# State scan of a four-layer convolution kernel: v*B on TensorE from diagonal images of B, the decay in SBUF

## What is computed

```
delta = softplus(dt_proj(x_proj(xi)) + bias)          # (2, 4, 192, 2304)
A     = -exp(A_log)                                   # (4, 192, 16)
h[n, l] = exp(delta[l] * A[n]) * h[n, l-1] + f(S[l], A[n]) * v[l] * B[n, l]
y[l]    = sum over n of C[n, l] * h[n, l]
```

## Time and profile before

| | us |
|---|---|
| median of three runs (2942.47 to 2949.4) | 2945.18 |
| span of the profiled execution, first to last instruction | 2938.3 |
| VectorE busy | 2503.6 |
| TensorE busy | 2263.7 |
| GpSimd busy | 1896.0 |
| ScalarE busy | 1743.5 |

### The profile page before, as it was taken

How to read it: one execution, slowest core, us unless ns; L and a number is a source line. 1 busy time by engine, 2 the same in 40 slices (tenths; PEclk the granted TensorE clock), 3 DMA queues, 4 the chain that set the end, 5 groups by cost and what they waited for, 6 DMA issues and landing times. The chain is left out here.

```text
span 2938.3 us, 27688 instructions
## 1 busy us (share of the span) xinstructions
PE 2263.7 (77%) x8714; PEld 1197.9 (41%) x8714; DVE 2503.6 (85%) x2085; ACT 1743.5 (59%) x2935; POOL 1896.0 (65%) x646
## 2 busy tenths in 40 slices
PE   6853677777877777787777778778984999799579
PEld 3421234343443434343443434444442555355444
DVE  5657999999999999999999999986787777699721
ACT  1566787878888888888878788863230000263220
POOL 0166999999999999999999999984000000198000
PEclk9967799999999999999999999998997999899689
DMA  1277445555454555545455554535005453100360
GB/s 48 88 219 272 102 112 137 130 124 130 115 133 118 131 136 123 129 112 132 119 131 134 125 129 112 135 90 191 0 0 143 110 129 104 43 8 8 82 89 24
DMA packets 145457, 323.07 MB, mean 110 GB/s; under 512 B 48219, under 2 KB 63840, under 8 KB 140320
## 3 DMA queue, kind: packets, MB, share of 16 engines
q1 hardware_dynamic: 144224, 317.17, 42.7%
q10 hardware_dynamic: 1088, 4.13, 0.6%
HBM read 234.46 MB, written 46.87 MB: 96 GB/s over the span
## 5 line engine op out<-in xcount | busy, mean ns | idle before, releaser
L903 POOL TENSOR_TENSOR l0c_r<-l0c_r,l0c_v 128x1536 f32<-128x1536 f32 x253 | 869.4, 3442 | 96.3 <-DVE l0c_r L862 96.3
L940 ACT ACTIVATE ps<-l0c_dlt,l0c_na 128x512 f32<-128x512 f32 (+1 forms) x1152 | 625.5, 574 | 286.5 <-DVE l0c_h L891 267.2
L912 POOL TENSOR_TENSOR l0c_hcp<-l0c_cb,l0c_h 128x1536 f32<-128x1536 f32 x216 | 743.2, 3446 | 5.5 <-DVE l0c_h L891 4.1
L891 DVE TENSOR_TENSOR_SCAN l0c_h<-ps,l0c_h,l0c_r 128x768 f32<-128x768 f32 x384 | 694.1, 1808 | 1.8 <-issue 1.2
L818 PE MATMUL ps<-l0c_hcp,net_ident 128*128 128x512 f32 x1728 | 645.2, 496 | 25.2 <-ACT l_Z L933 11.9
L950 ACT ACTIVATE l0c_r<-l0c_S,l0c_floor,l0c_na 128x768 f32<-128x768 f32 x576 | 579.9, 1014 | 0.1
L862 DVE SCALAR_TENSOR_TENSOR l0c_r<-l0c_r,ps 128x768 f32<-128x768 f32 x576 | 536.1, 931 | 18.1 <-issue 8.5
L752 PE MATMUL ps<-l0c_Bp,l0c_sel 96*128 96x512 bf16 x1012 | 256.0, 335 | 301.1 <-DVE l0c_hcv L869 146.1
L818 PEld LDWEIGHTS ps<-l0c_hcp,net_ident 128*128 128x128 f32 x1728 | 299.2, 193 | 297.6 <-issue 216.9
L891 DVE TENSOR_TENSOR_SCAN l0c_h<-ps,l0c_r 128x768 f32<-128x768 f32 x192 | 335.4, 1747 | 0.0
L1628 PE MATMUL ps<-l_prod,l_wa 128*96 128x384 f32 (+1 forms) x888 | 292.1, 493 | 25.7 <-DVE l_prod L1545 25.7
(11 more groups left out here) (280 smaller groups left out, 2739.9 us busy)
## 6 DMA issues: line engine op xcount, KB each, us to landing
l0c_cb<-cf SPq DMA_DIRECT2D x432, 384.0 KB, 5.5
l_other<-l_p SPq DMA_DIRECT2D x22, 864.0 KB, 6.0
dlt<-l0s_dl SPq DMA_DIRECT2D x36, 384.0 KB, 2.3
v<-l0s_vv SPq DMA_DIRECT2D x36, 384.0 KB, 2.9
l0c_dlt<-dlt SPq DMA_DIRECT2D x36, 384.0 KB, 3.6
l0c_v<-v SPq DMA_DIRECT2D x36, 384.0 KB, 4.4
l_other<-l_p SPq DMA_DIRECT2D x22, 288.0 KB, 6.7
l0c_Bp<-bc SPq DMA_DIRECT2D x36, 144.0 KB, 3.8
```

What stands on the lines that cost most here:

```text
L891: dve.tensor_tensor_scan(h[:, n, :], da[j % 2], r[:, j % NR, :], init, ALU.mult, ALU.add).then_inc(s_scan, 1)
L903: pool.tensor_tensor(two, two, v[:, (j // N) % 2, :].unsqueeze(1).to_broadcast([128, 2, SEG]), ALU.mult).then_inc(s_w, 2)
L912: pool.tensor_tensor(hcp[:, p % NHP:p % NHP + 2, :], cb[:, p % NCB:p % NCB + 2, :], h[:, e % N:e % N + 2, :], ALU.mult).then_inc(s_hp, 2)
L940: act.activation(da[e % 2][:, part], dlt[:, i, part], ACT.Exp, scale=na[:, i, n:n + 1]).then_inc(done, 1)
```

## The change

**Scan.** A step is now two states by 64 channels: partitions 0 to 63 hold state 2g and 64 to 127 state 2g+1, of the first or the second half of a tile's channels (s). The units go through the three tiles of a segment before the next segment. v is turned by TensorE (`turn`, three parts a unit) and copied to SBUF by ScalarE (`empty`). GpSimd makes images of B: diagonal 64x64 blocks, 12 a state pair, by a product of B's column values with an identity, both broadcast (`image`, 128x768; 192 in all, 11 ahead of the loop). TensorE multiplies turned v by the images (`v_b`, 24 matmuls of 64x64 by 64 columns a step), so PSUM receives v*B and `times_v` goes. All products with C are on GpSimd (288, two steps each). `add_y` sums the two states of a tile with 64-column weights. The decay goes to three SBUF places, in one instruction. b_r runs one step ahead of the scan. The last column of h is kept by ScalarE (`carry`). SP loads C rows per pair, two DMAs, for the middle tile four, and S beside delta and v.

**Steps.** S is computed here by VectorE (36 scans, second input in PSUM) and stored; B is computed in turned form and stays in SBUF (`BC`), C is computed once for all directions; the bf16 parts, their splitting and their DMAs go. v is stored in image order for the reversed directions.

```diff
+            for i in range(U + 2):
                 if i < U:
                     g, t, k, c0 = place(i)
                     sp.wait_ge(s_dl, i + 1)
                     sp.dma_start(d["dlt"][g, :, c0:c0 + SEG], dl[:, i % ND, :]).then_inc(s_dst[i % ND], 16)
...
+                    sp.wait_ge(s_vv, i + 1)
+                    vc = L - SEG - c0 if k % 2 else c0
+                    sp.dma_start(d["v"][g, :, vc:vc + SEG], vv[:, i % ND, :]).then_inc(s_vst[i % ND], 16)
+                if i >= 2:
+                    g, t, k, c0 = place(i - 2)
+                    sp.wait_ge(s_sum, i - 1)
+                    sp.dma_start(d["S"][g, :, c0:c0 + SEG], So[:, (i - 2) % ND, :]).then_inc(s_sst[(i - 2) % ND], 16)
+                if i == NC // 2 + 3:
+                    sp.wait_ge(s_bce, NC)
+                    for r in range(K * B):
+                        k, b = divmod(r, B)
+                        sp.dma_start(d["cf"][k, 3 * b:3 * b + 3, :, :].rearrange("r n l -> n r l"),
+                                     cr[N * r:N * r + N, :].unsqueeze(1).to_broadcast([N, 3, L])).then_inc(s_out, 16)
...
+                    k, j = divmod((q - NC) * GRP, NCH)
+                    if k >= 2:
+                        pe.wait_ge(s_xt, T)
+                    for i in range(GRP):
+                        for t in range(T):
+                            x = XT[:, t, :] if k >= 2 else XI[:, t, :]
+                            x = halves(x[:, (j + i) // 6 * SEG:((j + i) // 6 + 1) * SEG])
+                            for y in range(2):
+                                mm = pe.matmul(ps[64 * y:64 * y + 64, o + 32 * i:o + 32 * i + 32], x[:, y, (j + i) % 6, :],
+                                               w_b[:, k, t, :], start=(t == 0), stop=(t == T - 1))
...
+            def running_sum(i, idle):
+                if i % UN:
+                    dve.wait_ge(s_sum, i)
+                    init = So[:, (i - 1) % ND, SEG - 1:SEG]
+                else:
+                    init = 0.0
+                dve.wait_ge(s_dl, i + 1)
+                if i >= ND:
+                    dve.wait_ge(s_sst[i % ND], 16 * (i // ND))
+                dve.tensor_tensor_scan(So[:, i % ND, :], dl[:, i % ND, :], idle, init, ALU.add, ALU.bypass
+                                       ).then_inc(s_sum, 1)
...
+        G = N // 2
+        NR, NH, NHP, NG, NI, ND = 6, 3, 3, 3, 11, 3
+        LATE, LAG = 5, 4
+        TURN, EMPTY, STORE = (5, 7, 9), (11, 13, 15), LAG + 6
...
+        img = sb("img", [128, NI, 2, 6, 64])
+        h = sb("h", [128, NH, 2, SEG])
+        last = sb("last", [128, T, G, 2])
+        hc = sb("hc", [128, NHP, 2, SEG])
+        cb = sb("cb", [128, NG, 2, SEG])
+        da = sb("da", [128, ND, SEG])
...
+        PB, PV, PY = (0, BANK), 2 * BANK, 3 * BANK
...
+        def batch(t, s):
+            return (2 * t + s) // 3
...
+            for p in range(J // 2):
+                u, g = divmod(p, G)
+                t, k, c0 = place(u)
+                if p >= NG:
+                    sp.wait_ge(s_hc, p - NG + 1)
+                for s in range(2 if t == 1 else 1):
+                    for x in range(2):
+                        sp.dma_start(cb[64 * x:64 * x + 64, p % NG, s, :],
+                                     d["cf"][k, 2 * t + s, 2 * g + x, c0:c0 + SEG].unsqueeze(0).to_broadcast([64, SEG])
+                                     ).then_inc(s_cb[p % NG], 16)
+                if g == (0 if u == 0 else 1) and u + 1 < U:
...
+            def v_b(j):
+                u, n = divmod(j, N)
+                g, s = divmod(n, 2)
+                q = image_of(j)
+                pe.wait_ge(s_vt, 3 * u + 3)
+                pe.wait_ge(s_img, q + 1)
                 if j:
...
+                    pe.wait_ge(s_r, j)
+                for c in range(6):
+                    for half in range(2):
+                        rows = slice(64 * half, 64 * half + 64)
+                        o = PB[half] + 64 * (5 - c if place(u)[1] % 2 else c)
+                        for x in range(2):
+                            mm = pe.matmul(ps[64 * x:64 * x + 64, o:o + 64], vT[rows, u % 2, c, 64 * s:64 * s + 64],
+                                           img[rows, q % NI, x, c, :], start=True, stop=True)
+                mm.then_inc(s_vb, 1)
...
+            def turn(u, part):
+                if part == 0:
+                    pe.wait_ge(s_v, 16 * (u + 1))
+                if u or part:
+                    pe.wait_ge(s_vt, 3 * u + part)
+                for c in range(2):
+                    for x in range(2):
+                        mm = pe.matmul(ps[64 * x:64 * x + 64, PV + 128 * c:PV + 128 * c + 128],
+                                       halves(v[:, :])[:, x, 2 * part + c, :], ident[:, :], start=True, stop=True)
...
+            def add_y(p):
+                u, g = divmod(p, G)
+                if g == 0 and u:
+                    pe.wait_ge(s_evac, u)
+                pe.wait_ge(s_hc, p + 1)
+                for lo, hi in pieces(PY):
+                    for s in range(2):
+                        mm = pe.matmul(ps[64 * s:64 * s + 64, lo:hi], places[:, 0, :], hc[:, p % NHP, s, lo - PY:hi - PY],
+                                       start=(g == 0), stop=(g == G - 1))
...
+                if n in TURN and u + 1 < U:
+                    turn(u + 1, TURN.index(n))
+                if j + 1 < J:
+                    v_b(j + 1)
+                if j >= LATE and (j - LATE) % 2:
+                    add_y((j - LATE) // 2)
...
+                dve.wait_ge(s_vb, j + 1)
+                rj = r[:, j % NR, :].rearrange("p (h x) -> p h x", h=2)
+                dve.scalar_tensor_tensor(rj, rj, 1.0, blocks(j), ALU.add, ALU.mult).then_inc(s_r, 1)
...
+                if j + 1 < J:
+                    b_r(j + 1)
+                dve.wait_ge(s_decay, j + 1)
+                dve.wait_ge(s_r, j + 1)
+                if j // 2 >= NH:
+                    dve.wait_ge(s_hc, j // 2 - NH + 1)
+                    dve.wait_ge(s_last, j // 2 - NH + 1)
+                if c0:
+                    dve.wait_ge(s_last, (u - T) * G + g + 1)
+                init = last[:, t, g, s:s + 1] if c0 else 0.0
+                dve.tensor_tensor_scan(h[:, j // 2 % NH, s, :], da[:, j % ND, :], r[:, j % NR, :], init, ALU.mult, ALU.add
...
-                dve.tensor_tensor_scan(h[:, n, :], da[j % 2], r[:, j % NR, :], init, ALU.mult, ALU.add
...
-            def times_v(j):
...
-                    pool.wait_ge(s_in[(j // N) % 2], (j // N // 2 + 1) * (16 * NLOAD))
-                pool.wait_ge(s_ub, j + 2)
-                two = r[:, j % NR:j % NR + 2, :]
-                pool.tensor_tensor(two, two, v[:, (j // N) % 2, :].unsqueeze(1).to_broadcast([128, 2, SEG]), ALU.mult
...
+            def image(q):
+                ks, m = divmod(q, 2 * G)
+                b, g = divmod(m, G)
+                k, seg = divmod(ks, NSEG)
+                if k % 2:
+                    seg = NSEG - 1 - seg
+                if q >= NI:
+                    pool.wait_ge(s_vb, steps_with(q - NI))
+                rows = BC[:, k, seg, b, 2 * g:2 * g + 2, :].rearrange("p n c -> p (n c)").unsqueeze(2)
+                pool.tensor_tensor(img[:, q % NI, :, :, :].rearrange("p n c t -> p (n c) t"),
+                                   rows.to_broadcast([128, 12, 64]),
+                                   places[:, k % 2, :].unsqueeze(1).to_broadcast([128, 12, 64]), ALU.mult
+                                   ).then_inc(s_img, 1)
+            def times_c(p):
+                t = place(p // G)[0]
+                pool.wait_ge(s_scan, 2 * p + 2)
+                pool.wait_ge(s_cb[p % NG], c_loads(p))
                 if p >= NHP:
...
-                    times_v(j)
...
+                    pool.wait_ge(s_y, p - NHP + 1)
+                rows = cb[:, p % NG, :, :] if t == 1 else \
+                    cb[:, p % NG, 0, :].unsqueeze(1).to_broadcast([128, 2, SEG])
+                pool.tensor_tensor(hc[:, p % NHP, :, :], rows, h[:, p % NH, :, :], ALU.mult).then_inc(s_hc, 1)
+            for q in range(NI):
+                image(q)
+            for p in range(J // 2):
+                ks, at = divmod(p, T * G)
+                times_c(p)
+                if G <= at < G + 5:
+                    image(2 * G * ks + at + 3)
+                elif at >= G + 5 and ks + 1 < K * NSEG:
+                    image(2 * G * (ks + 1) + at - G - 5)
...
-            def decay(e, part, done):
-                i, n = (e // N) % 2, e % N
-                act.activation(da[e % 2][:, part], dlt[:, i, part], ACT.Exp, scale=na[:, i, n:n + 1]
...
+            def decay(e):
+                u, s = e // N, e % 2
+                if e % N == 0:
+                    act.wait_ge(s_in[u % 2], (u // 2 + 1) * (16 * NLOAD))
+                if e >= ND:
+                    act.wait_ge(s_scan, e - ND + 1)
+                act.activation(da[:, e % ND, :], dlt[:, u % 2, s, :], ACT.Exp, scale=na[:, 0, column(e)]
+                               ).then_inc(s_decay, 1)
...
```

(8 more changed lines are left out.)

541 lines of the change are left out of this document (161 added, 380 removed).

## The result

The changed kernel takes 3629.1 us, the median of 4 runs (3625.0 to 3634.4), against 2947.3 for the kernel before in the same runs (2942.5 to 2952.5): the ratio is 1.231, interval 1.2289 to 1.2332. It is slower by some 682 us; 3655 (3450 to 3900) was forecast. Its profiled execution has a span of 3632.5 us, 694 more than that of before.

A forecast was written before the change was run, and what follows sets the result against it. VectorE and GpSimd were both taken as full in the scan stage. Turns between them +673 us, start +10 and steps stage +25 make +708 on 2945.2, say 3655 us (3450 to 3900).

The forecast's parts named there:

- Steps 1 and 4: Scan stage: scans with two SBUF inputs take turns with GpSimd; pairs of 8.44 or 7.64 us, +673 us.
- Step 3: GpSimd in the scan stage: 192 images of 128x768 at 1.81 us each, ends 0.83 and 3.0 us.
- Step 5: TensorE in the scan stage: v_b takes 1.51 us, hidden; a lower clock could add up to 144 us.
- Steps 6 to 8: Scan stage: ScalarE's work and the DMA loads stay hidden; the start costs +10 us, tail as now.
- Step 9: Steps stage: VectorE's 36 running sums take 61 us, partly absorbed by 62 us of idle time; +25 us.
- B: Scan stage: scans take no turns with GpSimd and four TensorE tiles run at once; 2841 us, 9% chance.

The follow-up runs named there:

- e2: The kernel before with only the decay moved from PSUM to two SBUF places, all else as it was; 3871.7 us, ratio 1.311.
- e10: The changed kernel, decay still in three SBUF places, with e8's order of turns, empties, stores and cut y pieces; 3599.7 us, ratio 1.2208.
- e8: The changed kernel with decay in two PSUM places, turns, empties and y stores rescheduled, earlier y in pieces of at most 256 columns; 2932.0 us, ratio 0.9952.
- e4: The changed kernel with the 24 v*B matmuls reordered, one row half after the other, so neighbours use two tiles, not four; 3712.8 us, ratio 1.2566.
- e9: e8 with v*B in 12 matmuls of 128 columns a step instead of 24 of 64, every second chunk's weights left out; 2845.1 us, ratio 0.9663.

## Why the prediction was right, and where its terms were off

The mechanism held: e2 has it alone, and e10 against e8 prices it. That 3655 lies only 26 us above the measured 3629 is in part luck, as misses of both signs cancel. Span against span, +708 was said and +694 came: the scans +642 instead of +673, the steps stage +55 instead of +25, the start -5 instead of +10, the tail +2 instead of 0. The terms, by the prediction's steps:

- *Steps 1 and 4, the turns.* Scans are recorded near 4.4 and 2.1 us, where 4.2 and 2.5 were said. A pair with an image takes 8.04 us (said: 8.44), one without 7.76 (7.64). The image was mis-sized, the hand-over too: a product ends 3.54 us after the scan, not 3.36, since it starts 0.08 behind the scan's end instead of 0.09 ahead; a scan then needs 1.61, not 1.71. The 0.09 was a misreading of the earlier trace rows. GpSimd was never idle there, and that product started when GpSimd's own product before it ended, at 1949.33:

```profile
1945.88 3.45 POOL L903 TENSOR_TENSOR l0c_r<-l0c_r,l0c_v 128x1536 f32<-128x1536 f32 x1
```

  So it had no scan to wait for, and the row has no hand-over in it. The errors partly cancel: 181 x 8.04 + 107 x 7.76 = 2286, against 2345 said; the 28 us up to the measured 2314 lie in the 75 pairs in which b_r waited.
- *Step 3, the image.* Taken as 1.81, 1.66 of it behind a scan; measured 1.44 alone (the first three are recorded as 4.33 us) and 1.27 behind a scan. So the lower end of 0.83 and the upper of 3.0 were both far off, and the product of the earlier trace rows was still a quarter too dear: here reading an element again and again cost nothing extra.
- *Step 5, TensorE.* v_b was put at 1.34 + 0.17 us, two tiles at once; it takes 0.93, which is (0.93 - 0.17)/48 = 16 ns a record and near the low end of 14. Hidden, so it moved nothing. The lower clock, up to 144 us in the range, came (0.77 in the scans) and cost at most about the 44 us for which b_r waits. The Trainium skill ("TensorEngine Tiling (Array Packing)", Tiling Modes) has four independent 64x64 tiles; the trace agrees, by 0.93 against the 1.44 us of e4.
- *Steps 6 to 8.* ScalarE and the C loads stayed hidden. The start was said to cost 10 us and gained 5. The images, cheaper than said, were not in its way: the first two b_r waited for ScalarE. And with b_r one step ahead only two b_r stand ahead of the first scan, 3.7 us from the first b_r's start, where a running sum and five b_r took 12.8.
- *Step 9, the steps stage: by share the largest miss.* "The idle 62 us takes part of it" failed: VectorE's busy time rose by 58.8 us, and its idle time in the stage hardly fell, from 62.2 to 58.5. Two thirds of the idle time (39 us) lie in the first 70 us of the stage, where VectorE waits for ScalarE; then comes one wait for a store. Its waits between 60 and 345 us:

```profile
DVE l0s_dl L541 <- ACT l0s_e L488: 40.3, 9, 9.4
DVE l0s_dl L541 <- DMA dlt<-l0s_dl: 11.7, 1, 11.7
```

  Behind that store, from 214 us on, it works without a gap, four instructions and 4.43 us a unit:

```profile
289.25 0.95 DVE L541 SCALAR_TENSOR_TENSOR l0s_dl<-ps,l0s_e 128x768 f32<-128x768 f32 x1
290.11 0.95 DVE L546 SCALAR_TENSOR_TENSOR ps<-l0s_u,ps 128x768 f32<-128x768 f32 x1
291.10 1.81 DVE L531 TENSOR_TENSOR_SCAN l0s_So<-l0s_dl,l0s_So,ps 128x768 f32<-128x768 f32 x1
292.83 0.93 DVE L552 SCALAR_TENSOR_TENSOR l0s_dl<-ps,l0s_dl 128x768 f32<-128x768 f32 x1
```

  The +25 should have been near the upper bound of 61: the stage measured +55.

Of the rivals, B (2841 us, no turns and four tiles) comes close to e8, in which the turns are gone: four tiles do run at once, and VectorE alone sets 2 x 2.57 = 5.14 us a pair. e8's scans take 1610.5 us instead of B's 1533, which is about the 70.9 us of stops, and the steps stage adds the rest. e9, at 2845, has neither stops nor turns.

## What to carry to other kernels

Before an operand moves from PSUM to SBUF, count the SBUF inputs of every VectorE instruction that reads it, and what GpSimd reads in the meantime: here one operand's place was worth 668 us of 3600, and with it in PSUM and the order mended the whole change gained 15 us (e8). Where such turns can't be avoided, add up the instructions of both engines as one chain, price the hand-over by their ends, and cut them so that work without the conflict lies beside each. Idle time in a stage takes an added instruction only where it lies between that stage's late instructions; the sum of idle time over the stage doesn't tell.
